# The value projection of the next group behind a tile's weighted values on TensorE

## What is computed

```python
x = x + tanh(g_xattn[0]) * L0_xattn(layernorm(x), ctx, ctx, Wq, bq, Wk, bk, Wv, bv, Wo, bo)
x = x + tanh(g_ffn[0])   * L0_ffn(layernorm(x), ...)      # a mixture of 4 experts
x = x + tanh(g_xattn[1]) * L1_xattn(layernorm(x), ctx, ctx, mask, ...)
x = x + tanh(g_ffn[1])   * L1_ffn(layernorm(x), ...)      # quantised, with a convolution

def L0_xattn(query, key, value, ...):                     # L1 the same, with a mask
    q = split_heads(query @ Wq.T + bq)
    k = split_heads(key @ Wk.T + bk)
    v = split_heads(value @ Wv.T + bv)
    attn = softmax(einsum('bhsd,bhtd->bhst', q, k) / sqrt(8))
    out = einsum('bhst,bhtd->bhsd', attn, v)
    return merge_heads(out) @ Wo.T + bo
```

## Time and profile before

| | |
|---|---|
| median of 3 runs | 946.1 us (946.05 to 946.44) |
| profiled execution, its own time | 948.64 us |
| its span | 946.9 us |
| granted TensorE clock, mean | 0.992 |
| busy PE / PEld | 97% / 78% |
| busy DVE / ACT / POOL | 85% / 81% / 70% |

### The profile page before, as it was taken

One profiled execution on the slowest core, in us unless ns is written; L12 is line 12 of the kernel. 1 busy time (PEld: TensorE's weight loads), 2 busy tenths in 40 slices (PEclk: granted clock), 3 DMA queues, 4 the chain that ended last, 5 costly groups with the idle time before them and its releaser, 6 DMA issues. The chain is left out here.

```text
span 946.9 us, 32706 instructions
## 1 busy us (share of the span) xinstructions
PE 915.8 (97%) x11654; PEld 738.8 (78%) x11654; DVE 809.3 (85%) x2348; ACT 765.4 (81%) x1675; POOL 665.6 (70%) x1254
## 2 busy tenths in 40 slices
PE   6999999999989999999899999999999999999996
PEld 3888788877879999998786777778777777777774
DVE  6888898899968898899788888888888869999996
ACT  5888888888877777786666887887888889999995
POOL 5787777776535556556978867676775558999883
PEclk9999999999999999999999999999999999999998
DMA  3501011100000000000000000000000003333333
GB/s 115 186 25 47 25 47 40 32 25 14 14 1 2 1 1 2 1 1 2 1 13 13 15 25 13 26 13 26 13 17 11 3 14 76 76 76 75 74 72 81
DMA packets 54272, 31.17 MB, mean 33 GB/s; under 512 B 38368, under 2 KB 46816, under 8 KB 54112
## 3 DMA queue, kind: packets, MB, share of 16 engines
q1 hardware_dynamic: 54112, 29.08, 11.6%
HBM read 16.48 MB, written 4.19 MB: 22 GB/s over the span
## 5 line engine op out<-in xcount | busy, mean ns | idle before, releaser
L995 DVE TENSOR_REDUCE smax<-score 128x16 f32<-128x1024 f32 x128 | 156.7, 1224 | 63.6 <-DVE a_st L990 38.9
L1363 PEld LDWEIGHTS bank<-vb,prob_t 128*64 128x64 f32 x4096 | 130.2, 138 | 49.8 <-issue 41.8
L1004 DVE TENSOR_TENSOR prob<-score,smax 128x512 f32<-128x512 f32 x256 | 164.8, 685 | 0.8
L642 ACT ACTIVATE prob_t<-bank 128x512 f32<-128x512 f32 x256 | 139.1, 595 | 19.8 <-PE bank L1338 6.1
L637 ACT ACTIVATE prob<-prob 128x512 f32<-128x512 f32 x256 | 147.5, 631 | 5.5 <-DVE prob L1004 5.5
L1363 PE MATMUL bank<-vb,prob_t 128*64 128x18 f32 x4096 | 142.5, 212 | 0.2
L1338 PE MATMUL bank<-const,prob 128*128 128x128 f32 x1024 | 133.3, 273 | 0.7 <-DVE x_all L1105 0.7
L1338 PEld LDWEIGHTS bank<-const,prob 128*128 128x128 f32 x1024 | 115.8, 141 | 1.6 <-DVE x_all L1105 1.1
L721 ACT ACTIVATE eb_t<-eb,gwt 128x128 f32<-128x128 f32 x256 | 81.4, 390 | 34.2 <-POOL eb_acc L494 21.5
L648 ACT ACTIVATE o_t<-bank,b_col 128x128 f32<-128x128 f32 x128 | 48.8, 381 | 65.5 <-PE bank L1338 65.2
L428 POOL TENSOR_SCALAR kj<-k_sb,const 128x512 f32<-128x512 f32 x124 | 85.6, 698 | 21.7 <-issue 21.7
(11 more groups left out here) (169 smaller groups left out, 2343.3 us busy)
## 6 DMA issues: line engine op xcount, KB each, us to landing
ctx_t<-in_ctx SPq DMA_DIRECT2D x32, 256.0 KB, 2.6
x_all<-in_x SPq DMA_DIRECT2D x16, 256.0 KB, 3.5
out_x<-x_all SPq DMA_DIRECT2D x64, 64.0 KB, 1.8
ew<-in_ew SPq DMA_DIRECT2D x2, 512.0 KB, 5.9
q2t<-q2b SPq DMA_TRANSPOSE x64, 2.4
f_cw<-in_f_cw SPq DMA_DIRECT2D x1, 768.0 KB, 7.0
w_t<-in_w_attn SPq DMA_DIRECT2D x2, 256.0 KB, 4.7
f_w<-in_f_w SPq DMA_DIRECT2D x2, 256.0 KB, 6.2
```

The lines of the kernel that those rows point to most:

```text
L642: act.activation(prob_t[:, 4 * half:4 * half + 4, :].rearrange("p i q -> p (i q)"), bank[(PT, PT2)[half]], ACT.Copy).then_inc(s["p_copied" ...
L995: dve.tensor_reduce(smax[:].rearrange("p (r h) -> p r h", r=RH), sc, AX.X, ALU.max).then_inc(s["smax_done"], 1)
L1004: dve.tensor_tensor(prob[:, par, half * 512:(half + 1) * 512].rearrange("p (r h k) -> p r h k", r=2, k=S), sc[:, g], m.unsqueeze(3).to_bro ...
L1363: last = pe.matmul(bank[OV][q, i * 2 * VW:(i + 1) * 2 * VW], prob_t[:, i, q], vb[:, k // G, v0 + b * NPAIR + i, :, :].rearrange("p h v -> ...
```

## The change

`project_v` of a step with j = 2, and the wait for `q_ready` in front of it, are moved from the end of the step (behind the transposes of `prob`) to the place behind `values` and ahead of `project_o`. Steps t = 2, 6, ..., 58 have it, 15 in each layer. Nothing else moves; the lists of DVE, ACT, POOL and SP are the same.

```diff
                     if has(-2):
                         values(n - 2, (k - 2) % 8)
+                    if j == 2 and has(2):
+                        wait(pe, "q_ready", n + 2 + G)
+                        project_v(L, 1 - gpar, bank[FRONT])
                     if has(-4):
                         project_o(L, n - 4)
                     if has(-3):
@@
                             wait(pe, "xn_lo_done", parts_done(L, n + 3))
                             project_parts(0, xn_hi, xn_lo, "q_mm")
-                    if j == 2 and has(2):
-                        wait(pe, "q_ready", n + 2 + G)
-                        project_v(L, 1 - gpar, bank[FRONT])
```

## The result

The changed kernel takes **950.26 us** (median of 11 runs, 947.35 to 956.97) where the kernel before takes 946.1 (11 runs beside them, 944.18 to 948.01): a ratio of 1.0048, 95% interval 1.0031 to 1.0065. It is 4.2 us slower. The forecast was 950.5.

A forecast was written before the change was run, and what follows sets the result against it. PE, busy throughout the groups of both layers, was taken as the bound. First layer 4.2 us plus second layer 0.25 made +4.4, from 946.1 to 950.5 us; 8-in-10 range 945.8 to 954.8.

The forecast's parts named there:

- The wait for q_ready: First layer, moved projection: PE stands 0.22 us for ACT's copy of the queries; no wait in the second layer.
- P: Start of PE's transposes of prob, from which ACT's chain counts; predicted 1.04 + 0.22 us later in the first layer.
- The wait for v_ready: First layer, transposes of a_xn: PE waits 0.20 us for ACT's copies of v; no wait in the second layer.
- The seam: PE, weighted values to next scores around the moved block: a gain of 0.05 us at each of 29 places.
- The disturbed groups: First layer, three groups from t = 46 to 54: DVE set-up work hides most of the shift, 0.1 us in all.
- The two ends: Ends of both layers, ACT's late copy of o delays DVE's division: +0.7 us in the first, +0.95 in the second.
- The sum: Whole kernel: first layer 4.2 us and second layer +0.25, together +4.4 us, giving 950.5 us.
- the first group: First layer, t = 2, with no projection of o in its step and DVE ahead: a loss of 0.1 us.
- The ten groups with the two waits: First layer, undisturbed groups: each 0.33 us longer, 3.3 us in all.
- Rival A: First-layer waits for q_ready and v_ready do not bite, leaving seam and second-layer end: 945.6 us; chance 0.14.
- B: Scores slip in under the last transposes, each seam gaining 0.22 us: 940.7, or 948.2 with first-layer waits; chance 0.08.
- C: Seam between two blocks of small matmuls costs 0.15 us at each of 29 places: 955.5 us; chance 0.14.

The follow-up runs named there:

- e5: Changed kernel with ACT's copy of the queries put ahead of the exponentials of its step: 947.83 us against 946.33 for the kernel before.
- e7: Changed kernel with one spare 128 x 128 copy on ACT ahead of the copies of v: 954.3 us, ratio 1.0084 to the kernel before.
- e2: Kernel before with the value projection moved in the second layer alone: 945.62 us against 945.92 for the kernel before.
- e3: Kernel before with the projection moved in the second layer alone, except its last group (t = 58): 944.46 us against 945.92.
- e12: Changed kernel with both small DVE set-up operations moved to steps where POOL is idle: 949.88 us against 945.94 for the kernel before.
- e11: Changed kernel with the projection left in its old place at t = 58 of both layers: 949.5 us against 946.5 for the kernel before.
- e4: Kernel before with the projection moved behind the output projection and the transpose of o_n, both layers: 954.94 us, ratio 1.0093.
- e1: Kernel before with the value projection moved in the first layer alone: 950.9 us against 945.92 for the kernel before.
- e10: Kernel before with DVE's thresholds operation put behind the statistics and their wait in the same step: 947.09 us against 946.5.
- e6: Changed kernel with ACT's copies of v put at the head of the step: 963.55 us, ratio 1.0176 to the kernel before.
- e8: Kernel before with one spare 128 x 128 copy on ACT ahead of the copies of v: 947.87 us against 946.33.
- e9: Changed kernel with DVE's thresholds operation one tile later: 950.82 us against 946.5 for the kernel before.

## Why the prediction was right, point by point

**The wait for q_ready: right in place, 0.08 off in its parts.** The start is at 1.18 and not 1.26. I counted 0.14 from the end of ACT's row to a matmul; load and matmul both start 0.05 behind it (132.20 to 132.25). What PE loses is nevertheless as predicted: without the wait the block starts at 0.95 (e5), and 1.18 - 0.95 = 0.23 against my 0.22. Both ends were 0.08 too late, so P is 1.21 later (2.69 behind the weighted values instead of 1.48) and not 1.26.

**The wait for v_ready: right.** P + 4.14 against P + 4.13, and the dose of e7 goes through one to one. The four transposes then take 0.56 and not 0.53, so the scores come at P + 4.70 and not 4.66. The group of 15.56 came out as forecast because this and the earlier P cancel. e5 is the clean test of the sum of two waits: take one away and the other stays.

**The seam: right sign, half its size.** Taken as 0.05, measured as 16.52 - 16.41 = 0.11. The failed step is "the block itself takes what 32 records of the same size take behind the weighted values, 1.04". 1.04 is the way from the weighted values to a projection of 128 x 128; from them to the block it is 0.96, from the block to the projection 577.79 - 576.73 = 1.06, and the scores follow P in 0.97. The three now make 2.99, where the earlier trace rows have 1.04 + 2.05 = 3.09. Over 15 places it made -1.65 instead of -0.7 over 14; the seam of the last step (t = 58) had been left out. The rule of the Trainium skill that the prediction weighs (page TensorE: Matmul & The Clock Gate, What overlaps and what doesn't), that a weight load overlaps matmuls in flight only where the row group differs, would have made each seam dearer; e2 and e3 show it cheaper by 0.11.

**The disturbed groups: wrong.** "Set-up work on DVE, which hides most of the shift" did not hide it: 1.08 for three groups where 0.1 was taken and 0 to 1.0 allowed. Three ordinary groups would cost 0.99. e12, without the two held operations, shows 0.71 from tile 43 to 55: the set-up work hid 0.28, and not 0.9. And the move itself made two of these operations longer, since they now start behind one of POOL: 1.08 - 0.71 = 0.37. How the 0.71 falls on the steps I can't say further than that 0.28 of it comes at tile 55.

**The two ends: right.** 0.69 against 0.7, and 0.91 against 0.95, both shown by e11 and the second by e3 as well (the way to DVE in the earlier trace rows is 0.10 and not 0.09, which changes nothing).

**The sum** is right to 0.2 because two errors cancel: the seam gave 0.95 more than thought and the disturbed groups took 0.98 more; the first group and the ends came out 0.26 lower together. That part of the agreement is luck. The ten groups with the two waits, 3.3 of the 4.2 us, are not. The forecast of the profiled execution, 953.0 with a span of 951.3, was missed (950.84 and 949.0): it took over a kernel before with two dips of the clock in the experts, and the execution that was profiled after has one. Rival A (no waits) is excluded by the rows and by e5 and e7. B (the scores slip under the transposes) is excluded: 0.97, not 0.8. C (a dearer seam) did not occur in the changed kernel, but one place further down it does: e4 has the 0.15 per group in the second layer. In the first layer its group lasts 15.58, where C would have 15.71; that its time (954.94) lies near C's 955.5 is partly chance.

## What to carry to other kernels

A block of independent work on the busiest engine is moved for free only if the buffer it fills is already empty and the copy that it releases is not next in line: look up both distances in one undisturbed group, add the way of the signal, and compare them with the slack, since two waits of 0.2 us in each group cost most of the 5 us that the first layer lost. Ask of a change that moves work in a loop where it pays by the place and not by the loop: here 14 of 30 places gain, and leaving out the other 16 is the better kernel. And price a block with its new neighbours on both sides, since the same 32 matmuls cost 0.26 more behind a transpose than behind the weighted values.

## What the runs showed of the hardware that I had not expected

- A 128 x 3 `tensor_scalar` on DVE takes 0.22 us when it starts ahead of a 1.28 us operation of POOL, and 1.15 to 1.19 when it starts 0.11 to 0.15 behind it. All twelve experiments fit this: where POOL's L447 had begun (e1, e4, e5, e7, e10, e11) it was long, where it had not, or POOL was idle (e2, e3, e6, e8, e9, e12), it was short, with or without the change. A shift of a few tenths on PE decides it.
- The way from the end of ACT's row to the matmul that waits is not one number: 0.05 us for the value projection behind the copy of the queries (132.20 to 132.25), 0.15 for the transposes behind the copies of v (137.75 to 137.90), 0.14 in the earlier trace rows. From the end of DVE's L965 to the load of the weighted values it is 0.07 (748.53 to 748.60, and 139.48 to 139.55 in e6). No run tells why they differ.
- The granted clock falls from 1.00 to 0.50 (2.4 to 1.2 GHz) in up to four places: near 15 to 23 us, twice in the experts (270 to 280 and 462 to 477, down to 0.57 as a mean of 4 us), and, in all fourteen profiles, 2.4 to 4.9 us ahead of the last matmul. Each dip in the experts costs 1.6 us, the one near the start 0.6 (tile 0 to 3 is 0.67 quicker in the three profiles e4, e5 and e12 that lack it, and 0.1 in that of after, which has it); what the last one costs no run shows. Around the first dip of the experts PE is not full: it is busy for 3.54, 2.88 and 2.32 of 4 us before the clock is back. But a similar pattern in the changed kernel (4.00, 3.27, 1.83, 3.65) had no dip, so what decides it stays open; it is as large as most effects of this study, and shifts of single tiles were needed to see past it.
